# A two-layer adaLN transformer stack with a mixture of experts: the experts' down products turned round, their gate moved to VectorE and the residual add to GpSimd

## The chip, the cores and the metric

The kernel runs on one core of one Trainium2 chip. The metric is the device time of one execution in microseconds, lower is better. Inside the core work TensorE (PE, with its weight loads shown apart as PEld), VectorE (DVE), ScalarE (ACT), GpSimd (POOL) and SyncE (SP), which here only issues DMAs.

## The reference, cut to what matters

Thirty-two samples of 256 tokens with 128 features pass through two layers, each an attention and a feed-forward part with a residual around it. The change is in the feed-forward part of the first layer, a mixture of experts:

```
h = layernorm(x) * (1 + cb) + sb                       # cb, sb, gb: one row of 128 per sample
combine = router(h)                                    # 4 of 16 experts per token, weights
routed = sum over e of combine[:, e] * (relu(h @ up_w[e].T)**2 @ down_w[e].T)
shared = relu(h @ shared_up.T)**2 @ shared_down.T
x = x + gb * (routed + shared)                         # gb: the gate, per sample and feature
```

Each expert has 64 inner features, the shared expert 256, so there are 16*64 + 256 = 1280 inner features, or ten blocks of 128.

## The kernel before

The kernel is a row of stages, each a block with one hand-ordered instruction list per engine: a setup, `attention0` (prefix `a_`), `moe` (prefix `b_`), `attention1` (`c_`) and `mlp` (`d_`). The activations `x` stay in SBUF, a token on each partition: 64 tiles of 128 tokens by 128 features. The change touches `moe` alone.

`moe` makes `RUNS` = 16 runs `n`, each over two samples, that is 512 tokens or four tiles (`T4`). The features of these tokens stand on partitions after TensorE has turned them (`pe_front`), with the 512 tokens along the free axis. For each block `u` of the ten (0 and 1 are the shared expert, 2 to 9 the routed ones):

- `pe_up(n, u)`: one float32 product, the 128x128 up weights stationary, the 512 tokens moving, into one of four PSUM banks `pU`. A float32 product shows in the trace as two matmul records, each with a weight load of its own.
- `act_relu`, `act_square` (ScalarE): relu out of PSUM, then the square, into `q` (routed) or `a` (shared).
- `dve_weigh` (VectorE, routed blocks): `a = q * cwB`, where `cwB` holds each token's weight for the expert, spread over that expert's 64 partitions. These 2 MB per run come by DMA: VectorE writes `cwT`, SyncE sends it to DRAM (`by_expert`, four DMAs), waits for that to land, and fetches it back spread (`cwB`, four DMAs of 512 KB). `cwB` has two buffers.
- `pe_down(n, u)`: the down weights `dT` stationary, the 512 columns of `a` moving, added up over the ten blocks in the PSUM bank `pD`: features on partitions, tokens along the free axis.

After the tenth block ScalarE multiplies `pD` by the gate (`act_gate`, two instructions, one per sample, the gate as a per-partition scalar `c.mod[:, 0, 5, ...]`) into `og`; TensorE turns `og` back in four 128x128 transposes into `pB` (`pe_back`); VectorE adds `pB` to `x` (`dve_add`) and later measures mean and variance of the new `x` for the next layer norm (`dve_measure`, steps 1 and 2). `ln_scales` makes the reciprocal roots out of the variances.

The order on each engine is written out by hand and skewed: in pass `n` of the loop TensorE does the last three downs of run `n-1` between the first three ups of run `n`, then `pe_front(n+2)`, up 3, down 0, up 4, down 1, `pe_route(n+2)`, up 5, `pe_back(n-1)`, down 2, and so on in turns. `pe_down(n, 0)` waits until `pD` of run `n-1` has been read (`s_og`). On SyncE everything stands in one list: per run the `by_expert` DMAs, a wait, the `cwB` DMAs, and in run 2 also the loads of the last stage's weights (`ahead`).

Of the kernel before, what the change touches and what calls it, by code (L numbers as in the profile page):

```python
# [7 lines left out]
F32 = mybir.dt.float32  # L8
F16 = mybir.dt.float16
I32 = mybir.dt.int32  # L10
ALU = mybir.AluOpType
# [1176 lines left out]
def moe(nc, c, weights, ahead, halve, following, products):  # L1188
# [4 lines left out]
    with ExitStack() as ctx:  # L1193
# [31 lines left out]
        r, q, a = ([sb(f'{x}{k}', [P, W]) for k in range(4)] for x in ('r', 'q', 'a'))  # L1225
        og = sb('og', [D, W])
        pX, pR, pD, pB = (ctx.enter_context(nc.psum_tensor('b_p' + x, [P, BANK], F32)) for x in 'XRDB')
# [5 lines left out]
        s_up, s_r, s_sq, s_a, s_dn = (sem(x) for x in ('up', 'r', 'sq', 'a', 'dn'))  # L1233
        s_og, s_oT, s_st = (sem(x) for x in ('og', 'oT', 'st'))
        s_eT, s_pz, s_pT, s_pd, s_pm = (sem(x) for x in ('eT', 'pz', 'pT', 'pd', 'pm'))
        block = ctx.enter_context(nc.Block())

        @block.sync
        def _(sp):
            for n in range(RUNS):  # L1240
                sp.wait_ge(s_cT, n + 1)
                if n >= 1:
                    for part in s_cw:
                        sp.wait_ge(part, 2 * 16 * n)
                for t in range(T4):
                    sp.dma_start(by_expert[:, t, :], cwT[SQ * t:SQ * t + E, :, :].rearrange('e j r -> e (j r)')).then_inc(s_cd, 16)
# [40 lines left out]
        def pe_down(pe, n, u):  # L1287
            if u < ST:
                pe.wait_ge(s_sq, IT * n + u + 1)
            else:  # L1290
                pe.wait_ge(s_a, RT * n + u - ST + 1)
            if u == 0 and n >= 1:
                pe.wait_ge(s_og, n)
            t = weights_of(u)
            pe.matmul(pD[:, :], dT[:, t * D:(t + 1) * D], a[(IT * n + u) % 4][:, :], start=u == 0, stop=u == IT - 1).then_inc(s_dn, 1)  # L1295

        def pe_back(pe, n):
            pe.wait_ge(s_og, n + 1)
            if n >= 1:
                pe.wait_ge(s_st, ADD_STEPS * (n - 1) + 1)  # L1300
            for t in range(T4):
                last = pe.transpose(pB[:, t * P:(t + 1) * P], og[:, t * P:(t + 1) * P], c.id32[:, :])
            last.then_inc(s_oT, 1)

        @block.tensor
        def _(pe):
            for n in range(-2, RUNS + 1):
# [29 lines left out]
                if 0 <= n < RUNS:  # L1337
                    pe_up(pe, n, 5)
                if 0 <= n - 1 < RUNS:
                    pe_back(pe, n - 1)  # L1340
                if n == RUNS:
# [104 lines left out]

        def dve_add(dve, n):
            dve.wait_ge(s_oT, n + 1)
            add_to_x(dve, c, s_st, n, T4, pB[:, :])

# [4 lines left out]
        def _(dve):  # L1455
            dve.wait_ge(weights.s_loaded, 16 * MOE_LOADS)
            dve.wait_ge(s_km, 4)
            for n in range(-2, RUNS + 1):
                if 0 <= n - 1 < RUNS:
                    dve_weigh(dve, n - 1, 9)  # L1460
                if n == RUNS:
                    dve.wait_ge(s_st, ADD_STEPS * (RUNS - 1))
                    ln_scales(dve, c, s_ln, LN_STEPS, slice(0, TILES - T4))
                if n < 1 and n + 1 >= 0:
# [6 lines left out]
                elif 1 <= n < RUNS - 2:  # L1471
                    dve_normalise(dve, n + 2)
                if 1 <= n and n + 1 < RUNS:
                    dve_weights(dve, n + 1)
                if 0 <= n < RUNS:
                    dve_weigh(dve, n, 2)
                    dve_weigh(dve, n, 3)
                    dve_weigh(dve, n, 4)
                if 0 <= n - 1 < RUNS:
                    dve_add(dve, n - 1)  # L1480
                if 0 <= n < RUNS:
# [11 lines left out]
                if 0 <= n - 1 < RUNS:  # L1493
                    dve_measure(dve, n - 1, 2)
                if 0 <= n + 2 < RUNS:
                    dve_group_ranks(dve, n + 2)
# [40 lines left out]

        def act_gate(act, n):
            if n >= 1:
                act.wait_ge(s_oT, n)  # L1540
            act.wait_ge(s_dn, IT * (n + 1))
            for m in range(S2):
                last = act.activation(og[:, m * N:(m + 1) * N], pD[:, m * N:(m + 1) * N], ACT.Copy, scale=c.mod[:, 0, 5, n * S2 + m:n * S2 + m + 1])
            last.then_inc(s_og, 1)

        @block.scalar
        def _(act):
            for n in range(-2, RUNS + 1):
                if 0 <= n < RUNS:
# [4 lines left out]
                    act_relu(act, n, 2)  # L1554
                if 0 <= n - 1 < RUNS:
                    act_gate(act, n - 1)
                if n == RUNS:
# [17 lines left out]
                if 5 <= n < 5 + MLP_HALVES:  # L1575
                    halve(act, n - 5)
                if 0 <= n < RUNS:
                    act_square(act, n, 5)
# [11 lines left out]
        def _(gp):  # L1590
# [10 lines left out]
            gp.wait_ge(s_pz, 3)  # L1601
            attention1_spread(gp, following, products)


# [880 lines left out]
```

## Time and profile before

| | |
|---|---|
| time, median of 3 runs | 1916.07 us (1915.91 to 1919.06) |
| profiled execution | 1918.4 us, its span 1916.7 us |
| busy share of the span | PE 97%, PEld 68%, DVE 82%, ACT 75%, POOL 36% |
| stage `moe` | from about 884 to 1202.9 us of the span |
| granted clock of TensorE, mean | 0.986 |

The span is the time from the first to the last instruction in the profile. Busy time is the time in which an engine had at least one instruction in flight; a matmul's record includes its way through the array, so records of neighbouring matmuls overlap, and the rate is read from their starts.

### The profile page before, as it was taken

To read this page: it belongs to the slowest core of one execution; us is meant where nothing else is said; L and a number is where in the kernel's file an instruction comes from. 1 tells how busy PE (TensorE), PEld (TensorE's weight loads), DVE (VectorE), ACT (ScalarE), POOL (GpSimd) and SP (SyncE) were. 2 spreads that over 40 slices of the span, in tenths; PEclk is the share of its full clock that TensorE was granted. 3 is DMA by queue.
4 is the path that set the end of the run, shared out by engine and by line. 5 is a ranking of instruction groups with operands and counts; after the bars stand their busy time and mean duration, and the time that the engine had idled before them with its cause. 6 is when DMAs were issued, how large, how long until landed. Compare 5 with 4: busy or idle time off the path is not lost. (4 is left out here: it accounts for less than half of the span.)

```text
span 1916.7 us, 41298 instructions
## 1 busy us (share of the span) xinstructions
PE 1860.9 (97%) x14878; PEld 1297.1 (68%) x14878; DVE 1568.7 (82%) x3859; ACT 1437.4 (75%) x2026; POOL 684.3 (36%) x956
## 2 busy tenths in 40 slices
PE   7999999999999999998999999899999979999998
PEld 4788888888888888885444444677777754444443
DVE  7888888888888888865767775699999978888886
ACT  3888888888888888875677776566677766666665
POOL 2555656655656655551000000355555530000000
PEclk8999999999999999999999999999999989999999
DMA  3501111101111101111765544100000000000000
GB/s 101 130 19 29 29 29 29 29 18 26 29 29 29 29 21 23 27 23 39 169 142 114 121 105 87 45 2 2 2 2 2 2 2 6 12 17 12 12 17 17
DMA packets 62121, 75.68 MB, mean 39 GB/s; under 512 B 10480, under 2 KB 35168, under 8 KB 61792
## 3 DMA queue, kind: packets, MB, share of 16 engines
q1 hardware_dynamic: 61920, 73.03, 16.3%
q8 instruction: 122, 2.00, 0.4%
q14 instruction: 79, 0.65, 0.1%
HBM read 51.47 MB, written 4.77 MB: 29 GB/s over the span
## 5 line engine op out<-in xcount | busy, mean ns | idle before, releaser
L531 PE MATMUL a_pS<-qs,k 128*128 128x256 f16 x1536 | 415.3, 273 | 2.5 <-ACT th L1004 2.3
L551 PEld LDWEIGHTS a_pO<-va,pr 128*128 128x128 f32 x2048 | 312.6, 191 | 61.9 <-issue 58.4
L551 PE MATMUL a_pO<-va,pr 128*128 128x66 f32 x2048 | 322.0, 249 | 1.6 <-POOL pr L1086 1.1
L1004 ACT ACTIVATE th<-a_pS 128x1536 f32<-128x1536 f32 x128 | 185.4, 1449 | 89.7 <-PE a_pS L531 89.6
L531 PEld LDWEIGHTS a_pS<-qs,k 128*128 128x128 f16 x1536 | 223.5, 146 | 4.1 <-issue 2.2
L1978 ACT ACTIVATE c_pr<-c_pS 128x2048 f32<-128x2048 f32 x96 | 180.3, 1879 | 58.6 <-PE c_pS L1786 58.6
L2033 POOL TENSOR_SCALAR_AFFINE_SELECT c_pr<-c_pr 128x512 f32<-128x512 f32 x256 | 154.9, 635 | 180.1 <-DVE c_pr L1880 180.1
L1086 POOL TENSOR_SCALAR_AFFINE_SELECT pr<-pr 128x512 f32<-128x512 f32 x256 | 156.3, 634 | 176.0 <-ACT pr L1012 175.7
L1012 ACT ACTIVATE pr<-th 128x1536 f32<-128x1536 f32 x128 | 190.0, 1485 | 1.1
L797 DVE TENSOR_TENSOR qg<-a_pW,a_gam 128x512 f32<-128x512 f32 x192 | 131.8, 687 | 66.2 <-ACT sq L968 62.5
L867 POOL TENSOR_TENSOR qp<-qg,qp 128x1024 f16<-128x1024 f32 x64 | 139.2, 2175 | 126.7 <-ACT qp L980 126.7
L1097 POOL TENSOR_TENSOR as<-on 128x128 f32<-128x128 f32 x256 | 162.2, 635 | 55.9 <-DVE on L860 55.2
L553 PE MATMUL a_pO<-va,pr 128*128 128x66 f32 x1024 | 171.9, 249 | 0.0
L1295 PE MATMUL b_pD<-b_a,b_dn 128*128 128x512 f32 x320 | 165.8, 604 | 4.0 <-DVE b_a L1445 3.5
L553 PEld LDWEIGHTS a_pO<-va,pr 128*128 128x128 f32 x1024 | 157.0, 191 | 14.3 <-issue 14.3
L1285 PE MATMUL b_pU<-b_hT,b_un 128*128 128x512 f32 x320 | 163.7, 597 | 0.0
L1445 DVE TENSOR_TENSOR b_a<-b_q,b_cwB 128x512 f32<-128x512 f32 x128 | 87.8, 688 | 73.4 <-ACT b_q L1536 61.9
L1523 ACT ACTIVATE b_r<-b_pU 128x512 f32<-128x512 f32 x160 | 95.5, 597 | 68.5 <-PE b_pU L1285 68.5
L1880 DVE TENSOR_SCALAR c_pr<-c_pr 128x2048 f32<-128x2048 f32 x96 | 116.3, 1211 | 26.4 <-ACT c_pr L1978 26.4
L451 PE MATMUL a_pW<-a_wq,hT 128*128 128x512 f32 x256 | 132.4, 600 | 0.9 <-DVE qg L797 0.6
L2178 PE MATMUL d_pH<-d_a,d_h1T 128*128 128x512 f16 x512 | 122.1, 381 | 2.7 <-DVE d_a L2290 2.7
L968 ACT ACTIVATE sq<-a_pW 128x512 f32<-128x512 f32 x192 | 110.8, 596 | 15.3 <-PE a_pW L451 10.4
(267 smaller groups left out, 4245.6 us busy)
## 6 DMA issues: line engine op xcount, KB each, us to landing
b_cwB<-b_by_expert SPq DMA_DIRECT2D x64, 512.0 KB, 8.5
k<-k SPq DMA_DIRECT2D x128, 128.0 KB, 2.3
x<-in_L_attn_tokens_dram SPq DMA_DIRECT2D x8, 512.0 KB, 6.9
out_dram<-x SPq DMA_DIRECT2D x16, 256.0 KB, 2.3
mb<-a_by_sample SPq DMA_DIRECT2D x31, 128.0 KB, 3.3
d_h<-in_L_ffn_h_w_dram SPq DMA_DIRECT2D x2, 1024.0 KB, 8.3
c_gb<-c_by_sample SPq DMA_DIRECT2D x1, 2048.0 KB, 6.7
b_by_expert<-b_cwT SPq DMA_DIRECT2D x64, 8.0 KB, 1.5
```

The source lines that it names most:

```text
L531: last = pe.matmul(out, (k1, k2)[part][k][:, keys, h // G2, :], q, start=part == 0, stop=part == 1)
L551: last = pe.matmul(out, w[:, hh * N + t * P:hh * N + (t + 1) * P], v[:, 0, p, :], start=True, stop=t == 0)
L553: last = pe.matmul(out, w[:, HPG * N + hh * P:HPG * N + (hh + 1) * P], v[:, 1, p, :], start=False, stop=True)
L867: eng.tensor_tensor(to[:, t, :, DH:2 * DH], x.rearrange('p (h d) -> p h d', d=DH), to[:, t, :, 0:DH], ALU.subtract).then_inc(done, 1)
L1004: act.activation(th[:, :], pS[:, :], ACT.Tanh, scale=1.0 / SOFTCLAMP).then_inc(s_th, 1)
L1012: act.activation(pr[g % 2][:, :], th[:, :], ACT.Exp, scale=SOFTCLAMP * DH ** (-0.5)).then_inc(s_pr, 1)
L1086: last = gp.affine_select(out=own, in_=own, compare_op=ALU.is_ge, fill=0.0, base=0, pattern=[[0, HPG], [1, P]], channel_multiplier=-1)
L1097: gp.tensor_tensor(as_[:, :, p * DH:(p + 1) * DH], o[:, :, 0, :], o[:, :, 1, :], ALU.add).then_inc(s_as, 1)
L1285: pe.matmul(pU[(IT * n + u) % 4][:, :], uT[:, t, :], hT[n % 3][:, :], start=True, stop=True).then_inc(s_up, 1)
L1295: pe.matmul(pD[:, :], dT[:, t * D:(t + 1) * D], a[(IT * n + u) % 4][:, :], start=u == 0, stop=u == IT - 1).then_inc(s_dn, 1)
L1978: act.activation(pr[(3 * n + b) % NB][:, :, :], pS[:, :, :], ACT.Exp, scale=float(1.0 / np.sqrt(np.float32(DQ)))).then_inc(s_ex, 1)
L2033: gp.affine_select(out=part, in_=part, compare_op=ALU.is_ge, fill=0.0, base=0, pattern=[[0, HPG], [1, P]], channel_multiplier=-1).then_inc ...
```

## The change

The down product is turned round: the activations `a` become stationary, four tiles of 128 tokens each, and the down weights move, 128 columns. One `pe_down` is now four float32 products of 128 columns where it was one of 512; the sum in `pD` stands in token rows, as `x` does. `pe_back` and its transposes are gone. The gate is no longer one scalar per partition, but a row per sample along the free axis: TensorE turns the gates once (`pe_turn_gates`, in pass -1), ScalarE copies them (`act_take_gates`), SyncE sends them to DRAM at run 1 and fetches them per run spread over all partitions (`sp_load_gates`, 128 KB into `gr`, two buffers). VectorE multiplies `pD` by `gr` into `og` (`dve_gate`), and GpSimd adds `og` to `x` (`add`; the last run's is VectorE's). The `ln_scales` of the first 60 tiles moves behind the last measure.

```diff
-        og = sb('og', [D, W])
+        og = sb('og', [P, T4, D])
+        gates, gr = og[0:B, 0, :], [sb(f'gr{k}', [P, S2, D]) for k in range(2)]
+        GATES_OUT = 18
+        gate_rows = nc.dram_tensor('b_gate_rows', (B, D), F32, kind='Internal').ap()
...
+        def sp_load_gates(sp, n):
+            if n >= 2:
+                sp.wait_ge(s_og, n - 1)
+            sp.wait_ge(s_gr, GATES_OUT + 16 * n)
+            sp.dma_start(gr[n % 2][:, :, :].rearrange('p m d -> p (m d)'),
+                         gate_rows[n * S2:(n + 1) * S2].rearrange('m d -> (m d)').partition_broadcast(P)).then_inc(s_gr, 16)
...
             for n in range(RUNS):
+                if n == 1:
+                    sp.wait_ge(s_gr, 2)
+                    sp.dma_start(gate_rows, gates).then_inc(s_gr, 16)
+                    sp_load_gates(sp, 0)
+                if n >= 1:
+                    sp_load_gates(sp, n)
                 sp.wait_ge(s_cT, n + 1)
...
-            pe.matmul(pD[:, :], dT[:, t * D:(t + 1) * D], a[(IT * n + u) % 4][:, :], start=u == 0, stop=u == IT - 1).then_inc(s_dn, 1)
-
-        def pe_back(pe, n):
-            pe.wait_ge(s_og, n + 1)
-            if n >= 1:
-                pe.wait_ge(s_st, ADD_STEPS * (n - 1) + 1)
-            for t in range(T4):
-                last = pe.transpose(pB[:, t * P:(t + 1) * P], og[:, t * P:(t + 1) * P], c.id32[:, :])
-            last.then_inc(s_oT, 1)
+            for k in range(T4):
+                last = pe.matmul(pD[:, k * D:(k + 1) * D], a[(IT * n + u) % 4][:, k * P:(k + 1) * P], dT[:, t * D:(t + 1) * D],
+                                 start=u == 0 and k == 0, stop=u == IT - 1 and k == T4 - 1)
+            last.then_inc(s_dn, 1)
+
+        def pe_turn_gates(pe):
+            pe.transpose(pB[0:B, 0:D], c.mod[:, 0, 5, :], c.id32[:, :]).then_inc(s_gr, 1)
...
-        def dve_add(dve, n):
-            dve.wait_ge(s_oT, n + 1)
-            add_to_x(dve, c, s_st, n, T4, pB[:, :])
+        def dve_gate(dve, n):
+            dve.wait_ge(s_dn, IT * (n + 1))
+            dve.wait_ge(s_gr, GATES_OUT + 16 * (n + 1))
+            if n >= 1:
+                dve.wait_ge(s_st, ADD_STEPS * (n - 1) + 1)
+            dve.tensor_tensor(og[:, :, :].rearrange('p (m t) d -> p m t d', t=TT), pD[:, :].rearrange('p (m t d) -> p m t d', m=S2, t=TT),
+                              gr[n % 2][:, :, :].unsqueeze(2).broadcast_to((P, S2, TT, D)), ALU.mult).then_inc(s_og, 1)
+
+        def add(eng, n):
+            eng.wait_ge(s_og, n + 1)
+            if n >= 1:
+                eng.wait_ge(s_st, ADD_STEPS * n)
+            xt = c.x[:, n * T4:(n + 1) * T4, :]
+            eng.tensor_tensor(xt, xt, og[:, :, :], ALU.add).then_inc(s_st, 1)
...
-        def act_gate(act, n):
-            if n >= 1:
-                act.wait_ge(s_oT, n)
-            act.wait_ge(s_dn, IT * (n + 1))
-            for m in range(S2):
-                last = act.activation(og[:, m * N:(m + 1) * N], pD[:, m * N:(m + 1) * N], ACT.Copy, scale=c.mod[:, 0, 5, n * S2 + m:n * S2 + m + 1])
-            last.then_inc(s_og, 1)
...
             attention1_spread(gp, following, products)
+            for n in range(RUNS - 1):
+                add(gp, n)
```

On TensorE the middle of a pass reads as follows before the change; `b_pU` is an up product, `b_pD` a down, `b_pX` the turned tokens of the run after next, `b_pR` the router's product and `b_pB` the back transposes.

```order
L1266 MATMUL b_pX<-id,b_xn 128x128 x4
L1285 MATMUL b_pU<-b_hT,b_un 128x512
L1295 MATMUL b_pD<-b_a,b_dn 128x512
L1285 MATMUL b_pU<-b_hT,b_un 128x512
L1295 MATMUL b_pD<-b_a,b_dn 128x512
L1276 MATMUL b_pR<-b_hT,b_gT 32x128 x4
L1285 MATMUL b_pU<-b_hT,b_un 128x512
L1302 MATMUL b_pB<-id,b_og 128x128 x4
L1295 MATMUL b_pD<-b_a,b_dn 128x512
```

The same place of the changed kernel:

```order
L1282 MATMUL b_pX<-id,b_xn 128x128 x4
L1301 MATMUL b_pU<-b_hT,b_un 128x512
L1312 MATMUL b_pD<-b_dn,b_a 128x128 x4
L1301 MATMUL b_pU<-b_hT,b_un 128x512
L1312 MATMUL b_pD<-b_dn,b_a 128x128 x4
L1292 MATMUL b_pR<-b_hT,b_gT 32x128 x4
L1301 MATMUL b_pU<-b_hT,b_un 128x512
L1312 MATMUL b_pD<-b_dn,b_a 128x128 x4
```

The four transposes are gone, and each down stands as four products of 128 columns at the place of the one of 512.

On VectorE, at the start of a pass before the change, `b_xn` is the normalised run after next, `b_cw` to `b_cwT` the expert weights of the next run, `b_a` the weighing:

```order
L112 TENSOR_SCALAR b_xn<-x,mv,rs 128x128 x4
L1425 SCALAR_TENSOR_TENSOR b_cw<-b_rep,b_s 128x64
L1427 TENSOR_REDUCE b_tot<-b_cw 128x4
L1429 TENSOR_SCALAR b_tot<-b_tot 128x4
L1431 RECIPROCAL b_tot<-b_tot 128x4
L1433 SCALAR_TENSOR_TENSOR b_cwp<-b_cw,b_tot 128x4x16
L1437 STREAM_TRANSPOSE b_cwT<-b_cwp 128x128
L1445 TENSOR_TENSOR b_a<-b_q,b_cwB 128x512 x3
L128 TENSOR_TENSOR x<-x,b_pB 128x512
```

In the changed kernel:

```order
L112 TENSOR_SCALAR b_xn<-x,mv,rs 128x128 x4
L1466 TENSOR_TENSOR b_og<-b_pD,b_gr 128x512
L1439 SCALAR_TENSOR_TENSOR b_cw<-b_rep,b_s 128x64
L1441 TENSOR_REDUCE b_tot<-b_cw 128x4
L1443 TENSOR_SCALAR b_tot<-b_tot 128x4
L1445 RECIPROCAL b_tot<-b_tot 128x4
L1447 SCALAR_TENSOR_TENSOR b_cwp<-b_cw,b_tot 128x4x16
L1451 STREAM_TRANSPOSE b_cwT<-b_cwp 128x128
L1459 TENSOR_TENSOR b_a<-b_q,b_cwB 128x512 x4
```

The gate stands ahead of the six instructions that make `cwT`, so these now come after the wait for the last down; the add behind the third weighing is gone.

On SyncE the first runs before the change:

```order
L1246 DMA b_by_expert<-b_cwT 16x128 x4
L1253 DMA b_cwB<-b_by_expert 64x4x512 x4
L1246 DMA b_by_expert<-b_cwT 16x128 x4
L1253 DMA b_cwB<-b_by_expert 64x4x512 x4
L1246 DMA b_by_expert<-b_cwT 16x128 x4
L1253 DMA b_cwB<-b_by_expert 64x4x512 x4
```

And in the changed kernel:

```order
L1262 DMA b_by_expert<-b_cwT 16x128 x4
L1269 DMA b_cwB<-b_by_expert 64x4x512 x4
L1253 DMA b_gate_rows<-b_og 32x128
L1245 DMA b_gr<-b_gate_rows 128x256 x2
L1262 DMA b_by_expert<-b_cwT 16x128 x4
L1269 DMA b_cwB<-b_by_expert 64x4x512 x4
L1245 DMA b_gr<-b_gate_rows 128x256
L1262 DMA b_by_expert<-b_cwT 16x128 x4
L1269 DMA b_cwB<-b_by_expert 64x4x512 x4
```

Ahead of run 1's expert weights now stand the gate rows' way out and two fetches, each of which waits for the one before it to land; ahead of every later run's stands one fetch.

## Rows read from the trace of the kernel before

**Rows 1.** Windows: us, then each engine's busy time, TensorE clock, DMA share

```profile
908.00:916.00 8.00, 6.59 (x9) 2.80 (x10) 6.30 (x20) 2.43 (x4) 0.00 (x0) 0.57 0.54 106
1008.00:1026.00 18.00, 18.00 (x56) 8.10 (x55) 12.94 (x53) 13.62 (x26) 0.00 (x0) 1.00 0.62 129
```

**Rows 2.** Timeline, TensorE, one pass: start, duration, engine, line, operation

```profile
1014.14 1.02 PE L1295 MATMUL b_pD<-b_a,b_dn 128*128 128x512 f32 x2
1015.00 0.60 PE L1266 MATMUL b_pX<-id,b_xn 128*128 128x128 f32 x4
...
1020.30 0.60 PE L1302 MATMUL b_pB<-id,b_og 128*128 128x128 f32 x4
1020.74 1.02 PE L1295 MATMUL b_pD<-b_a,b_dn 128*128 128x512 f32 x2
...
1033.62 0.60 PE L1266 MATMUL b_pX<-id,b_xn 128*128 128x128 f32 x4
```

**Rows 3.** Timeline, ScalarE and VectorE, the same pass

```profile
1015.26 0.84 ACT L1543 ACTIVATE b_og<-b_pD,mod 128x256 f32<-128x256 f32 x2 [0.32 <-PE b_pD L1295]
...
1012.48 1.11 DVE L112 TENSOR_SCALAR b_xn<-x,mv,rs 128x128 f32<-128x128 f32 x4
1013.50 0.22 DVE L1425 SCALAR_TENSOR_TENSOR b_cw<-b_rep,b_s 128x64 f32<-128x64 f32 x1
...
1016.65 0.69 DVE L1445 TENSOR_TENSOR b_a<-b_q,b_cwB 128x512 f32<-128x512 f32 x1 [1.65 <-ACT b_q L1536]
```

**Rows 4.** Timeline, TensorE in attention1: two products of 128 columns in turn

```profile
1307.66 0.63 PEld L1775 LDWEIGHTS c_pC<-c_wv,c_hT 128*128 128x128 f32 x4
1307.87 0.61 PE L1775 MATMUL c_pC<-c_wv,c_hT 128*128 128x128 f32 x4
```

**Rows 5.** Timeline, SyncE's queue: start, time to issue, DMAs

```profile
913.28 1.71 SPq L1246 DMA_DIRECT2D b_by_expert<-b_cwT  x4
916.06 2.56 SPq L1253 DMA_DIRECT2D b_cwB<-b_by_expert  x4
...
954.03 2.57 SPq L1253 DMA_DIRECT2D b_cwB<-b_by_expert  x4
...
1017.80 2.56 SPq L1253 DMA_DIRECT2D b_cwB<-b_by_expert  x4
```

**Rows 6.** DMA issues: KB each, median us from issue to landing

```profile
mb<-a_by_sample SPq DMA_DIRECT2D x31, 128.0 KB, 3.3
```

**Rows 7.** Timeline, VectorE and TensorE, runs 1 and 3: weighings that waited for cwB

```profile
923.66 0.69 DVE L1445 TENSOR_TENSOR b_a<-b_q,b_cwB 128x512 f32<-128x512 f32 x1 [2.03 <-DMA b_cwB<-b_by_expert]
...
961.95 1.44 DVE L1445 TENSOR_TENSOR b_a<-b_q,b_cwB 128x512 f32<-128x512 f32 x2 [3.35 <-DMA b_cwB<-b_by_expert]
...
927.20 0.60 PE L1302 MATMUL b_pB<-id,b_og 128*128 128x128 f32 x4
...
964.44 0.60 PE L1302 MATMUL b_pB<-id,b_og 128*128 128x128 f32 x4
```

**Rows 8.** Groups by line, GpSimd: count, busy us, mean ns

```profile
L867 POOL TENSOR_TENSOR qp<-qg,qp 128x1024 f16<-128x1024 f32 x64 | 139.2, 2175 | 126.7 <-ACT qp L980 126.7
L128 POOL TENSOR_TENSOR x<-x,c_og 128x256 f32<-128x256 f32 x32 | 28.4, 887 | 5.1 <-DVE c_og L1914 5.1
```

**Rows 9.** Timeline, ScalarE and VectorE, end of the stage

```profile
1197.78 0.84 ACT L1543 ACTIVATE b_og<-b_pD,mod 128x256 f32<-128x256 f32 x2 [2.23 <-PE b_pD L1295]
...
1201.93 0.69 ACT L1676 ACTIVATE c_wq<-b_pU 128x16 f32<-128x16 f32 x4
...
1196.18 0.18 DVE L88 TENSOR_SCALAR var<-mv 128x60 f32<-128x60 f32 x1
...
1198.16 0.22 DVE L104 SCALAR_TENSOR_TENSOR rs<-ln_half,rs 128x60 f32<-128x60 f32 x1
1199.43 0.69 DVE L128 TENSOR_TENSOR x<-x,b_pB 128x512 f32<-128x512 f32 x1 [1.05 <-PE b_pB L1302]
...
1201.06 0.38 DVE L140 BATCH_NORM_AGGREGATE mv<-stat 128x2 f32<-128x6 f32 x4
```

More of the change, by code:

```diff
@@ L1233, in moe @@
         s_up, s_r, s_sq, s_a, s_dn = (sem(x) for x in ('up', 'r', 'sq', 'a', 'dn'))
-        s_og, s_oT, s_st = (sem(x) for x in ('og', 'oT', 'st'))
+        s_og, s_st, s_gr = (sem(x) for x in ('og', 'st', 'gr'))
         s_eT, s_pz, s_pT, s_pd, s_pm = (sem(x) for x in ('eT', 'pz', 'pT', 'pd', 'pm'))
         block = ctx.enter_context(nc.Block())
+        def sp_load_gates(sp, n):
[4 more added lines that the diff above has]
+                         gate_rows[n * S2:(n + 1) * S2].rearrange('m d -> (m d)').partition_broadcast(P)).then_inc(s_gr, 16)
         @block.sync
@@ L1338, in _ @@
                     pe_up(pe, n, 5)
-                if 0 <= n - 1 < RUNS:
-                    pe_back(pe, n - 1)
+                if n == -1:
+                    pe_turn_gates(pe)
                 if n == RUNS:
@@ L1460, in _ @@
                     dve_weigh(dve, n - 1, 9)
-                if n == RUNS:
-                    dve.wait_ge(s_st, ADD_STEPS * (RUNS - 1))
-                    ln_scales(dve, c, s_ln, LN_STEPS, slice(0, TILES - T4))
                 if n < 1 and n + 1 >= 0:
@@ L1472, in _ @@
                     dve_normalise(dve, n + 2)
+                if 0 <= n - 1 < RUNS:
+                    dve_gate(dve, n - 1)
+                if n == RUNS:
+                    add(dve, RUNS - 1)
                 if 1 <= n and n + 1 < RUNS:
@@ L1478, in _ @@
                     dve_weigh(dve, n, 4)
-                if 0 <= n - 1 < RUNS:
-                    dve_add(dve, n - 1)
                 if 0 <= n < RUNS:
@@ L1494, in _ @@
                     dve_measure(dve, n - 1, 2)
+                if n == RUNS:
+                    dve.wait_ge(s_st, ADD_STEPS * (RUNS - 1))
+                    ln_scales(dve, c, s_ln, LN_STEPS, slice(0, TILES - T4))
                 if 0 <= n + 2 < RUNS:
@@ L1536, in act_square, with act_take_gates @@
             act.activation(to[:, :], r[(IT * n + u) % 4][:, :], ACT.Square).then_inc(s_sq, 1)
-        def act_gate(act, n):
-            if n >= 1:
-                act.wait_ge(s_oT, n)
-            act.wait_ge(s_dn, IT * (n + 1))
-            for m in range(S2):
-                last = act.activation(og[:, m * N:(m + 1) * N], pD[:, m * N:(m + 1) * N], ACT.Copy, scale=c.mod[:, 0, 5, n * S2 + m:n * S2 + m + 1])
-            last.then_inc(s_og, 1)
+        def act_take_gates(act):
+            act.wait_ge(s_gr, 1)
+            act.activation(gates, pB[0:B, 0:D], ACT.Copy).then_inc(s_gr, 1)
         @block.scalar
@@ L1554, in _ @@
                     act_relu(act, n, 2)
-                if 0 <= n - 1 < RUNS:
-                    act_gate(act, n - 1)
                 if n == RUNS:
@@ L1576, in _ @@
                     halve(act, n - 5)
+                if n == -1:
+                    act_take_gates(act)
                 if 0 <= n < RUNS:
```

## The prediction

> **What bounds the kernel now.** The change touches one stage, so the first view is the table of busy time by stretch. In an 18 us stretch of the stage TensorE is busy for all 18.00 us at a granted clock of 1.00, while VectorE works 12.94, ScalarE 13.62 and GpSimd nothing [rows 1]. The second view is the timeline of one pass: from one group of `b_pX` transposes at 1015.00 to the next at 1033.62 it is 18.62 us, with no idle time on TensorE between [rows 2]. So the stage's length is the sum of what TensorE issues; an instruction taken from ScalarE or VectorE is worth nothing in itself, and one put on them costs nothing while its result is there when TensorE asks. The third view is SyncE's queue, since the waits for `cwB` in the first runs are the only ones near TensorE's needs [rows 5, 7].
>
> A record's duration must not be added up here, since records overlap: a down shows 1.02 us, but the next group starts 0.86 us after it (1014.14 to 1015.00), and that is what it costs. The four back transposes cost 1020.74 - 1020.30 = 0.44 us [rows 2].
>
> **The back transposes go.** Passes 1 to 15 hold one group each: 15 x 0.44 = **-6.6 us**. The sixteenth stands at the stage's end and is counted there.
>
> **The downs.** One down was two records of 512 columns and becomes eight of 128, each with a weight load of 128x128 float32. Before, the load hid behind the 512 columns of the record ahead. Now load and matmul are about equally long, and the question is what one costs next to the other. The nearest row is in attention1: four records of 128 columns with fresh float32 weights, not transposes, take 0.61 us from the first start to the last end, one record being 0.275 long, so they start every (0.61 - 0.275)/3 = 0.112 us; their loads show (0.63 - 0.19)/3 = 0.147, of which the first wait, for the 256-column record ahead, takes the excess [rows 4]. The transposes give (0.60 - 0.273)/3 = 0.109 us, as their own loads are lighter [rows 2]. I take 0.112, since it is the same operation in form and type: 8 x 0.112 = 0.896 against 0.86, or 0.036 more per down. For 160 downs that is **+5.8 us**. Below, 0.109 gives 0.872 and +1.9; above stands the case that nothing is hidden (second rival).
>
> **The gate on VectorE.** ScalarE began the gate at 1015.26 and needed 0.84 us [rows 3]. VectorE multiplies 512 columns in 0.69 [rows 3], with a source in PSUM too [rows 9], and is free from 1015.00 on, so it ends at about 1015.95, 0.15 us sooner. `pe_down(n, 0)`, which waits for it, loses nothing. Queued behind the gate are the six instructions for `cwT`, which took from 1013.50 to 1015.00 [rows 3] and now run from 1015.95 to 1017.45; then the weighing for down 2, done at 1018.15. TensorE asks for it where the transposes stood, 1020.30: 2.1 us of cover. `cwT` itself is 2.45 us late, and with the 128 KB gate fetch ahead of it `cwB` starts about 3 us later than 1017.80 [rows 5]; it is needed in the next pass, some 17 us on, and its first half comes within 7.6 us (below). **0**. ScalarE's lost 0.84 us were under TensorE: **0**.
>
> **The add on GpSimd.** GpSimd is idle here. Its two-input add takes 0.887 us for 256 columns and 2.175 for 1024 [rows 8], so some 1.3 for 512. `dve_measure` wants it only behind four weighings of 0.69 that start at 1017.45, so from 1020.2 on; the add is done by 1017.3: **0**. If its ports hold VectorE up while it runs, the weighing at 1018.15 slips to 1019.45, still before 1020.30: the hold decides from 2.1 us on. The Trainium skill ("SBUF — State Buffer", port pair shared by VectorE and GpSimd) says that a GpSimd instruction and a VectorE one with two SBUF inputs lock each other out fully; by that the slip is the whole add, and still zero in the sum.
>
> **The gate rows' way round.** This is the new wait. SyncE's list is in order. At run 1 it used to start the `by_expert` DMAs at 913.28, as soon as run 0's `cwB` had landed [rows 5]. Now three steps come first: `gate_rows` goes out, queued behind run 0's `cwB` and so landing at about that same moment, some 0.3 to 1 us later; the fetch of run 0's rows waits for it and lands, as the like 128 KB spread does, in 3.3 us [rows 6]; the second fetch is issued (0.6 us, as one of the four `cwB` DMAs in 2.56 [rows 5]) and the `by_expert` DMAs queue behind its data. Sum 4.2 us; bounds 3.0 (both landings short) and 5.0. So run 1's `cwB` starts at 920.3, not 916.06. VectorE's first weighing of run 1 was released 7.6 us after the issue, at 923.66 [rows 5, 7]; now 927.9, result at 928.6. TensorE wants it at 927.2 plus 0.2 for longer downs, where the transposes stood [rows 7]: a stall of 1.2 us.
>
> The queue then stays dense through the loads for the last stage: run 3's `cwB` was issued at 954.03, and its weighing began at 961.95 [rows 5, 7]. With 4.2 us inherited, the issue and data of two more fetches (1.1), and 0.74 for the weighing, the result is there at 968.0. TensorE wants it at 964.44, less two groups of transposes (0.9), plus 25 longer downs (0.9) and the 1.2 already lost: 965.6. A stall of 2.4. Both together are the inherited delay less 0.6: **+3.6 us** (2.4 to 4.4). By run 4 the queue has caught up, as each run's chain is shorter than a pass.
>
> **The end.** VectorE gates at 1197.78, where ScalarE did, to 1198.5, and adds. Add and measures took from 1199.43 to 1201.44, 2.0 us, so they end at 1200.5. The nine `ln_scales` steps, which were done at 1198.4 under the wait, now follow: 2.2 us, 1202.7. The other end of the stage, ScalarE's copies, was at 1202.6 and comes earlier, freed of the gate [rows 9]. **+0.1**. The one transpose of the gates falls in the start, where TensorE waits for the first `cwB` anyway (busy 6.59 of 8 us even as it ends [rows 1]): 0.
>
> **Sum.** -6.6 + 5.8 + 3.6 + 0.1 = +2.9; the gate's 0.15 us gives back a few hundredths per pass that down 0 now waits, -0.2 in all: **+2.7 us**. The profiled execution took 1918.4 us for a span of 1916.7, 2.3 above the median; the terms are differences and carry over, so the forecast is 1916.1 + 2.7 = **1918.8**, by the bound of 0.2% (3.8 us), which is about what a measurement of this kernel can tell from no change, the same.
>
> **Rivals.**
> *It gets faster (14%).* The fetches land early or the delay is used up by slack I don't see, and the records start every 0.109 us: -6.6 + 1.9 + 0 to 1 = -4.7 to -3.7, 1911.5 to 1912.5. For it: transposes at 0.109 all through this stage. Against it: both attention1 products, float32 weights, at 0.112, and the 3.3 us row. It decides if the stalls stay under 1 us.
> *The loads aren't hidden (4%).* A load of about 0.11 and a matmul of 0.107 in turn make 0.22 per record, 1.75 per down, +0.89 x 160 = +143 us, 2060. The attention1 rows speak against it: 0.112. The Trainium skill ("TensorE: Matmul & The Clock Gate", on what overlaps when small matmuls are packed) says that a load overlaps a matmul in flight only when its row group differs, and here all use the same rows; by that this rival would be the forecast. The trace disagrees, for these four records and for every down before.
> *The stall brings the clock down (24%).* After TensorE waited for run 0's `cwB`, the granted clock was 0.57 of full over 908 to 916 [rows 1]. If the 2.4 us stall in run 3 does the same, 8 us at 0.57 cost 8 x 0.43 = 3.4 us: 2.7 + 3.4 = +6.1, 1922.2, slower. For it: the stall is alike. Against: that wait was longer, with another one just before.
> *VectorE or the queue late in every pass (4%).* If GpSimd's hold goes past 2.1 us by 1, each pass loses 1: +15, 1933.
> The forecast itself: 54%.
>
> **From these the numbers.** The likeliest case alone spans 1913.8 (0.109 and short stalls: -6.6 + 1.9 + 2.4 = -2.3) to 1919.6 (long stalls, +0.8). The range reaches into the clock case: 1913.8 to 1923.2. Slower by over 0.2%: the clock, the loads, VectorE, 0.32. Faster 0.14. Same 0.54.
>
> **What the changed profile would show.** Eight records per down, starting every 0.112 us, and a steady pass of 18.62 - 0.44 + 0.36 = 18.5 us with TensorE still always busy; `cwB` of run 1 issued at about 920; TensorE waiting for `b_a` once in run 1 and once in run 3, 3.6 us together, and the clock row there at 1.00; GpSimd's add near 1.3 us; the stage's end set by `ln_scales`. The forecast fails if records start every 0.107 or 0.12, if the granted clock falls at run 3, or if each pass shows idle time on TensorE before down 2.

## The result and the profile after

The changed kernel took 1924.21 us (median of 20 executions, 1918.76 to 1932.34) against 1918.94 us for the kernel before in the same measurements (20, 1915.91 to 1925.48). The ratio is 1.0022, 95% interval 1.0012 to 1.0032: slower by 0.2%, about 4.2 us; the two medians lie 5.3 us apart, 0.27%, which is inside the interval. By the 4.2 us, added to the time before that the forecast started from (1916.07), it is 1920.3 us, in the upper half of the forecast range; the median of these 20 executions itself, which has a slower kernel before beside it, is 1.0 us above the range's end. Of the cases it is not the likeliest but the third rival, the one with the falling clock, and a second loss that the forecast did not have.

The profiled execution has a span of 1922.0 us, 5.3 more than before. Cut at TensorE's first record of the stage and at the first of the next one (`attention1`): 883.2 us before the stage instead of 884.7 (unchanged code; a second profile of the kernel before had 883.4), 323.3 in it instead of 318.2, and 715.4 behind it instead of 713.8.

The steady pass is the first thing to look at. Windows of the changed kernel (us, then busy time of PE, PEld, DVE, ACT and POOL with counts, TensorE's granted clock, DMA share, GB/s), one over a steady stretch, one over run 1 and one over run 3:

```profile
1008.00:1026.00 18.00, 18.00 (x110) 12.97 (x109) 14.11 (x57) 13.00 (x23) 1.27 (x1) 1.00 0.60 127
924.00:930.00 6.00, 4.71 (x34) 3.08 (x33) 3.38 (x7) 3.03 (x8) 0.00 (x0) 1.00 1.06 207
966.00:974.00 8.00, 5.93 (x26) 4.42 (x27) 5.57 (x18) 1.69 (x3) 0.00 (x0) 0.79 0.74 146
```

TensorE is as full as before in the steady stretch [rows 1], so the sum over its instructions still holds there. In run 1 and run 3 it is not full, and in run 3 its clock is below 1.00.

Timeline of TensorE in the changed kernel: a pass, and the two waits with what released them.

```profile
1020.00 0.60 PE L1282 MATMUL b_pX<-id,b_xn 128*128 128x128 f32 x4
...
1021.29 1.05 PE L1312 MATMUL b_pD<-b_dn,b_a 128*128 128x128 f32 x8
1022.18 1.02 PE L1301 MATMUL b_pU<-b_hT,b_un 128*128 128x512 f32 x2
...
1038.50 0.60 PE L1282 MATMUL b_pX<-id,b_xn 128*128 128x128 f32 x4
...
927.30 1.16 PE L1312 MATMUL b_pD<-b_dn,b_a 128*128 128x128 f32 x8 [1.29 <-DVE b_a L1459]
...
968.07 1.77 PE L1312 MATMUL b_pD<-b_dn,b_a 128*128 128x128 f32 x8 [3.49 <-DVE b_a L1459]
969.63 1.92 PE L1301 MATMUL b_pU<-b_hT,b_un 128*128 128x512 f32 x2
```

A pass is 18.50 us (1020.00 to 1038.50) where it was 18.62 [rows 2]; a down takes 1022.18 - 1021.29 = 0.89 us for eight records, 0.11 between starts: (1.05 - 0.28) / 7 = 0.11. The waits are for the weighed activations, 1.29 us in run 1 and 3.49 in run 3, and behind the second an up product shows 1.92 us where it has 1.02 at full clock. The pass with run 3's wait, from the `b_pX` at 959.06 to the one at 982.99, is 23.93 us long: 18.50, the wait of 3.49, and 1.94 more, most of it the lower clock (behind the wait of 1.29, where the clock stayed, the same difference is 0.3 us).

Why the weighing is late stands in SyncE's queue of the changed kernel (start, time to issue):

```profile
902.02 0.77 SPq L1253 DMA_DIRECT2D b_gate_rows<-b_og  x1
912.26 3.43 SPq L1245 DMA_DIRECT2D b_gr<-b_gate_rows  x2
915.80 1.75 SPq L1262 DMA_DIRECT2D b_by_expert<-b_cwT  x4
918.99 2.56 SPq L1269 DMA_DIRECT2D b_cwB<-b_by_expert  x4
...
931.45 1.96 SPq L1262 DMA_DIRECT2D b_by_expert<-b_cwT  x4
935.97 2.56 SPq L1269 DMA_DIRECT2D b_cwB<-b_by_expert  x4
...
959.66 2.56 SPq L1269 DMA_DIRECT2D b_cwB<-b_by_expert  x4
```

These stand beside [rows 5], where 1.5 us must be added to a start here, since the stage begins that much sooner. The gate rows are issued at 902.02, but the first fetch only at 912.26, when they have landed behind run 0's expert weights. These ten microseconds are not the price: `by_expert` of run 1 waits for run 0's `cwB` anyway, and started at 913.28 before the change, where the first fetch now starts at 912.26 + 1.5 = 913.7. The rest are the two fetches, one after the other, from 912.26 to 915.80. `by_expert` of run 1 starts at 915.80 + 1.5 = 917.3 instead of 913.28, 4.0 us late; `cwB` of run 1 at 920.5 instead of 916.06, of run 3 at 961.1 instead of 954.03, which is 7.1 us late.

VectorE and GpSimd in a steady pass, changed kernel:

```profile
1020.20 0.69 DVE L1466 TENSOR_TENSOR b_og<-b_pD,b_gr 128x512 f32<-128x512 f32 x1 [1.46 <-PE b_pD L1312]
...
1021.31 0.96 DVE L1443 TENSOR_SCALAR b_tot<-b_tot 128x4 f32<-128x4 f32 x1
...
1020.97 1.27 POOL L1474 TENSOR_TENSOR x<-x,b_og 128x512 f32<-128x512 f32 x1 [17.23 <-DVE b_og L1466]
```

The gate takes 0.69 us and the add 1.27, as forecast. The small `tensor_scalar` on four columns shows 0.96 us, and ends with GpSimd's add (1022.24). The `tensor_reduce` that began under the same add, at 1021.05, took its usual 0.22 us. No VectorE instruction with two inputs in SBUF begins under the add in a steady pass.

And the end of the stage, VectorE, ScalarE and TensorE of the changed kernel, then the windows behind the seam, one of the changed kernel and one of the kernel before:

```profile
1201.92 0.69 DVE L1474 TENSOR_TENSOR x<-x,b_og 128x512 f32<-128x512 f32 x1
...
1203.56 0.38 DVE L140 BATCH_NORM_AGGREGATE mv<-stat 128x2 f32<-128x6 f32 x4
...
1205.81 0.22 DVE L104 SCALAR_TENSOR_TENSOR rs<-ln_half,rs 128x60 f32<-128x60 f32 x1
...
1204.54 0.67 ACT L1701 ACTIVATE c_wq<-b_pU 128x16 f32<-128x16 f32 x4
...
1206.57 0.37 PE L1843 MATMUL c_pC<-id,mod 128*32 128x128 f32 x1 [3.63 <-PEq L1193]
```

```profile
1204.00:1217.00 13.00, 8.49 (x41) 6.08 (x42) 4.73 (x15) 2.41 (x19) 2.51 (x6) 0.50 0.39 163
```

```profile
1202.00:1209.00 7.00, 4.21 (x11) 2.89 (x11) 2.82 (x5) 1.45 (x10) 2.36 (x6) 0.51 0.46 190
1209.00:1216.00 7.00, 4.11 (x40) 3.12 (x38) 2.58 (x5) 2.46 (x3) 0.00 (x0) 1.00 0.27 112
```

ScalarE's copies end at 1205.2, `ln_scales` at 1206.0; TensorE waits 3.63 us for the next stage. Behind it the clock stands at 0.50 for all of 13 us; before the change it was back at 1.00 after 7.

### The profile page after: what moved, and what is told of

Same layout as the page of the kernel before. It is cut to its first block and busy times, and to the rows that moved or that the text cites. A ratio compares the mean times of both kernels' runs of the same rounds, so it can differ in the third digit from the quotient of the medians.

```text
span 1922.0 us, 43109 instructions
## 1 busy us (share of the span) xinstructions
PE 1861.8 (97%) x15775; PEld 1380.2 (72%) x15775; DVE 1577.7 (82%) x3860; ACT 1427.9 (74%) x1995; POOL 703.8 (37%) x971
## 5 line engine op out<-in xcount | busy, mean ns | idle before, releaser
L1312 PEld LDWEIGHTS b_pD<-b_dn,b_a 128*128 128x128 f32 x1280 | 170.2, 195 | 83.1 <-issue 62.5
L1312 PE MATMUL b_pD<-b_dn,b_a 128*128 128x128 f32 x1280 | 171.7, 279 | 8.2 <-DVE b_a L1459 8.2
```

The costliest lines, as they stand in the source:

```text
L1312: last = pe.matmul(pD[:, k * D:(k + 1) * D], a[(IT * n + u) % 4][:, k * P:(k + 1) * P], dT[:, t * D:(t + 1) * D], start=u == 0 and k == 0, ...
```

## The experiments

Ratios are to the kernel before in the same series of measurements, with 95% intervals; two versions of different series are compared by these ratios. "The wait" is TensorE's.

One thing must be known before the profiles are compared. In every version TensorE waits 2.8 to 4.2 us for run 0's expert weights, and behind that wait the clock is low for a time that varies from execution to execution. The five downs there, in e5 and in e6, which are the same kernel up to the seam (the place where `moe` ends and `attention1` begins):

```profile
907.63 7.65 PE L1313 MATMUL b_pD<-b_dn,b_a 128*128 128x128 f32 x40 [3.31 <-DVE b_a L1459]
908.45 6.36 PE L1313 MATMUL b_pD<-b_dn,b_a 128*128 128x128 f32 x40 [2.88 <-DVE b_a L1460]
```

They took 7.3 to 7.7 us in both profiles of the kernel before, in the changed kernel, e1, e2, e5 and e10, 6.9 to 7.2 in the changed kernel's second profile, e3 and e4, and 6.3 to 6.4 in e6 to e9. So a stage can be 1.3 us shorter by this alone, and TensorE then asks for run 3's weights that much sooner.

**e1: the gates early.** In SyncE's list:

```diff
-                if n == 1:
+                if n == 0:
                     sp.wait_ge(s_gr, 2)
                     sp.dma_start(gate_rows, gates).then_inc(s_gr, 16)
                     sp_load_gates(sp, 0)
-                if n >= 1:
+                    sp_load_gates(sp, 1)
+                if n >= 2:
                     sp_load_gates(sp, n)
```

with `pe_turn_gates` and `act_take_gates` moved to the start of the stage.

> The changed kernel, with the gates turned and copied at the start of the stage and their way to DRAM and the first two fetches issued before run 0's expert weights, where the queue is empty, instead of between run 0's and run 1's. Theory (the gate rows' way round delays the expert weights): TensorE's waits in run 1 (1.29 us) and run 3 (3.49 us) both go, and the granted clock stays at 1.00 through run 3 (it fell for 3.4 us, worth about 1.7): 6.5 us less than the changed kernel, so about -1.2 us against the kernel before (ratio 0.999). Steady pass unchanged at 18.50 us. Rival (the waits come from the later passes' fetches, or from expert weights computed later behind the gate): waits stay, time stays within 1 us of the changed kernel, ratio 1.002.

Measured: 1918.29 us against 1918.04, ratio 0.9999 (0.9988 to 1.0010). The intervals of this kernel and the changed one don't meet: the late gates cost 0.23%, some 4.4 us, where 6.5 had been expected. Windows of e1 over run 1, run 3 and behind the seam:

```profile
924.00:930.00 6.00, 6.00 (x43) 4.25 (x42) 3.99 (x13) 4.09 (x8) 0.00 (x0) 1.00 0.44 85
964.00:972.00 8.00, 8.00 (x46) 5.69 (x45) 7.31 (x36) 5.43 (x10) 0.00 (x0) 1.00 0.41 93
...
1197.00:1210.00 13.00, 7.78 (x39) 5.48 (x40) 5.26 (x15) 2.04 (x18) 2.36 (x6) 0.50 0.42 163
```

Both waits and the clock's fall are gone, the stage takes 316.7 us, 6.6 less than in the changed kernel and 1.5 less than before the change. VectorE's order with the gate ahead of the expert weights is unchanged here, so it is not what made the waits. But the kernel as a whole is not faster than before; behind the seam this profile has 717.3 us, at half clock for 13 us.

**e2: the fetches alone, in the kernel before.** The same DMAs at the same places of SyncE's list, from a cleared buffer into two that nobody reads:

```diff
+                if n == 1:
+                    sp.wait_ge(s_k, 2)
+                    sp.dma_start(gate_rows, gsrc[:, :]).then_inc(s_k, 16)
+                    sp_load_gates(sp, 0)
+                if n >= 1:
+                    sp_load_gates(sp, n)
                 sp.wait_ge(s_cT, n + 1)
```

> The kernel before, with the same DMAs as the changed one at the same places of SyncE's list (gate rows out at run 1, two fetches there, one per later run), into buffers that nobody reads; downs, gate and back transposes are as before. Theory: the queue alone makes the waits. TensorE's need is later here by the transposes (0.44 us a pass), so the wait in run 1 is about 0.9 us, in run 3 about 3.0, with or without the clock's fall: +4 to +6 us against before (ratio 1.002 to 1.003). Rival: the waits need the changed order on VectorE; then no wait and ratio 1.000.

Measured: 1925.72 us, ratio 1.0040 (1.0026 to 1.0054). In the profile the waits are 0.88 us in run 1, 0.62 in run 2 and 1.22 in run 3, 2.7 together (groups of waits: sum in us, count, longest):

```profile
PE b_pD L1310 <- DVE b_a L1460: 2.7, 3, 1.2
```

The queue alone makes waits, without any change on VectorE or TensorE. That in run 1 came as expected (0.9), that in run 3 did not (3.0 expected), and that in run 2 was not foreseen; the clock did not fall behind any of them. The time is larger than these waits and above what was expected: the stage is 3.7 us longer, and another 2.7 lie behind the seam, at a mean clock of 0.68 over 1203 to 1224 us. Why that part is there in this kernel, whose end of the stage is as before, stays open.

**e3: the downs in four, in the kernel before.** Stationary weights as before, loaded for each quarter:

```diff
-            pe.matmul(pD[:, :], dT[:, t * D:(t + 1) * D], a[(IT * n + u) % 4][:, :], start=u == 0, stop=u == IT - 1).then_inc(s_dn, 1)
+            for k in range(T4):
+                last = pe.matmul(pD[:, k * P:(k + 1) * P], dT[:, t * D:(t + 1) * D], a[(IT * n + u) % 4][:, k * P:(k + 1) * P],
+                                 start=u == 0 and k == 0, stop=u == IT - 1 and k == T4 - 1)
+            last.then_inc(s_dn, 1)
```

> The kernel before, each down product split into four of 128 columns with the same stationary weights, loaded anew for each; nothing else changed. Theory (a record of 128 columns is bound by its 0.112 us load): a down costs 0.89 us instead of 0.86, a pass 18.62 + 0.34 = 18.96 us, +5.5 us against before, ratio 1.0029. Rival (the cost belongs to the activations as stationary operand, or to short records' issue): if only activations as weights cost it, ratio 1.000; if it is issue, more than +6.

Measured: 1924.94 us, ratio 1.0042 (1.0030 to 1.0055). Its passes:

```profile
1018.25 0.60 PE L1266 MATMUL b_pX<-id,b_xn 128*128 128x128 f32 x4
...
1037.22 0.60 PE L1266 MATMUL b_pX<-id,b_xn 128*128 128x128 f32 x4
```

18.97 us, 0.35 more than 18.62, as expected: the price is that of short records with a float32 load each, not of activations as weights. It is 16 x 0.35 = 5.6 us of the 8 measured; the stage is 4.9 us longer in the profile (the five downs behind run 0's wait were 0.6 us shorter in this execution), and the remainder lies in unchanged stages, where this execution's clock was 0.53 over 11 us behind the seam. Whether it is the load or something else in a short record that sets the 0.112 us is not shown: a quarter of the 0.43 us of a 512-column record is 0.107, so what comes on top is 0.005 us a record.

**e4: the first two fetches together.** No wait for the first to land before the second is issued (`if n != 1` ahead of the wait in `sp_load_gates`, and the gate of run 0 waits for both).

> The changed kernel, with the second fetch of run 1 issued without waiting for the first to land. Theory: the delay of run 1's by_expert DMAs falls from about 4 us to about 1.5 (one landing of 2.3 us less), the wait in run 1 goes, that in run 3 shrinks from 3.49 to about 2.4 us or less (total waits = delay less a constant), 2.4 us less than the changed kernel, 4 if the clock no longer falls. Rival (the delay comes from the gate rows waiting behind run 0's expert weights, not from the fetches' landings): no difference.

Measured: 1923.27 us, ratio 1.0034 (1.0022 to 1.0046); the interval overlaps that of the changed kernel, so in time nothing is shown. The profile does answer. Run 1's `by_expert` starts 1.3 us later in the stage than before the change, not 4.0; there is no wait in run 1, one of 1.07 in run 3, and the clock there is at 1.00.

```profile
PE b_pD L1313 <- DVE b_a L1460: 1.1, 1, 1.1
```

The stage takes 317.2 us, 6.1 less than in the changed kernel, 3.7 of them waits and about 1.9 the clock in run 3, so the fetch's landing was the larger part of the delay. The same execution lost as much in unchanged code, 2.5 us ahead of the stage and 3.7 behind the seam, which is why the stage has to be read from the profile here.

**e5: as e1, with the scales at their old place**, `ln_scales` of the first 60 tiles ahead of the last gate.

> The changed kernel with the gates early, as in e1, and the ln_scales of the first 60 tiles back at their old place, right behind the last weighing and ahead of the last gate. Theory (the moved scales stretch the end of the stage, and with it TensorE's wait of 3.63 us at the seam to the next stage, which keeps the clock at half for longer there): the stage ends about 1.0 us earlier, the seam's wait is near 2.6 us, and the half-speed stretch after it is shorter than 13.7 us; 1 to 3 us less than e1, ratio 0.998 to 0.9995. Rival (the scales' place costs nothing, as ScalarE's copies end then anyway): ratio as e1, 1.000.

Measured: 1919.49 us, ratio 0.9995 (0.9983 to 1.0007). TensorE at the seam, and the windows behind it:

```profile
1198.53 0.37 PE L1842 MATMUL c_pC<-id,mod 128*32 128x128 f32 x1 [2.57 <-PEq L1193]
```

```profile
1197.00:1204.00 7.00, 4.32 (x11) 2.88 (x11) 2.77 (x10) 2.07 (x18) 2.51 (x6) 0.51 0.37 133
1204.00:1210.00 6.00, 4.03 (x40) 3.12 (x38) 2.59 (x5) 1.53 (x3) 0.00 (x0) 1.00 0.48 198
```

The wait is 2.57 again, the half-speed stretch 7 us again, and the profiled span 1911.7 against 1916.9 in e1. Over the timed executions the difference to e1 is 0.04%, less than the intervals: the shape at the seam is shown, its worth in time is not by this pair.

**e6 and e7: TensorE kept busy over the seam**, in e5 and in the kernel before:

```diff
                     attention1_multiply(pe, following, products, pU[1]).then_inc(s_pm, 1)
+                    keep_busy(pe, c, pU[2], 20)
```

> As e5, with 20 idle transposes of the identity on TensorE (2.2 us) behind its last products of the stage, while it would wait for the next stage; they write a bank that nobody reads. Theory (the half-speed stretch at the seam is what the rest of the kernel loses): the granted clock stays at 1.00 through the first products of attention1, or falls for one short stretch; 1.5 to 3.5 us less than e5, ratio against before about 0.997. Rival (the stretch is set by the waits inside attention1's first batch): same as e5.

> The kernel before, with the same 20 transposes at the same place. Theory: the seam's half-speed stretch (6.8 us before) goes too, 1 to 3 us less, ratio 0.9985 to 0.9995; the changed kernel loses more at this seam than the kernel before, so it gains more from them. Rival as in e6: 1.000.

Measured: e6 1916.31 us, ratio 0.9983 (0.9972 to 0.9994); e7 1918.75, ratio 1.0000 (0.9991 to 1.0009). Windows behind the seam, e6, then e7:

```profile
1197.00:1210.00 13.00, 8.68 (x69) 6.84 (x68) 6.51 (x19) 5.33 (x30) 2.51 (x6) 1.00 0.43 163
```

```profile
1200.00:1217.00 17.00, 12.15 (x76) 8.79 (x75) 6.35 (x11) 5.57 (x15) 4.32 (x9) 0.80 0.32 125
```

With the wait cut to 0.30 us the clock stays at 1.00 in e6. In the kernel before the same cut only moves the slow part: 0.80 over the 17 us, and no gain. So my expectation for e7 was wrong, and what e6 has over e5 is not settled as the seam's alone; the two intervals overlap. e6 shows a wait of 1.14 us in run 3 where e5 has none. That is no effect of the transposes: `cwB` of run 3 is issued 71.2 us into the stage in e6 and 71.3 in e5, but TensorE, after its shorter downs in run 0, began run 3's pass 1.2 us sooner.

**e8: as e1, with the add on VectorE** behind the third weighing.

> As e1, with the add on VectorE at its old place behind the third weighing of a pass instead of on GpSimd. Theory (VectorE is not asked for anything there by TensorE): VectorE's small tensor_scalar in the weights falls from 0.96 to 0.17 us, the pass stays at 18.50 us with TensorE always busy, time as e1, ratio 1.000. Rival (the move to GpSimd buys time): slower than e1 by up to 0.69 x 15 = 10 us, ratio 1.005.

Measured: 1920.48 us, ratio 1.0004 (0.9992 to 1.0016), as e1. VectorE's `tensor_scalar` and TensorE's passes:

```profile
1035.04 0.17 DVE L1443 TENSOR_SCALAR b_tot<-b_tot 128x4 f32<-128x4 f32 x1
```

```profile
1015.22 0.60 PE L1283 MATMUL b_pX<-id,b_xn 128*128 128x128 f32 x4
1033.73 0.60 PE L1283 MATMUL b_pX<-id,b_xn 128*128 128x128 f32 x4
```

0.17 instead of 0.96, and a pass of 18.51: the add on GpSimd holds VectorE up, and where it stands makes no difference to the time that this pair can tell. A wait of 1.83 us stood in run 3 of this profile, at a clock of 1.00.

**e9: as e6, each fetch behind its run's expert weights**, and VectorE's weights for the next run ahead of the gate.

```diff
-                if n >= 2:
-                    sp_load_gates(sp, n)
...
+                if n >= 2:
+                    sp_load_gates(sp, n)
                 if n == 2:
                     ahead(sp)
```

> As e6 (gates early, scales back, transposes over the seam), with each later run's gate fetch issued behind that run's expert weights instead of ahead of them, and on VectorE the weights of the next run ahead of the gate. Theory: in run 3 the expert weights no longer queue behind a fetch and come about 1.1 us earlier, so the wait of 1.14 us that e6 showed there goes, and none is left in the steady passes; up to 1.1 us less than e6, ratio 0.998 or just under. Rival (the wait in run 3 comes from the last stage's loads alone): as e6.

Measured: 1915.77 us against 1918.25, ratio 0.9978 (0.9966 to 0.9990), the lowest of all versions and clear of the kernel before, but with an interval that overlaps e6's. The run 3 wait is gone; two short ones for the gate came in its place in the early runs:

```profile
PE b_pD L1313 <- DVE b_og L1467: 0.8, 2, 0.6
```

`cwB` of run 3 was issued 0.8 us sooner than in e6, and the two short waits brought TensorE to it 0.5 us later, so both had a part. The edit also changed two things at once, the fetch's place and VectorE's order, and no run separates them.

**e10: the changed kernel with late gates, but the scales back and the seam closed.**

> The changed kernel with its late gates, but the scales at their old place and the 20 transposes over the seam. Theory (queue and seam are two separate losses that add): e6 plus the waits in runs 1 and 3 and the clock's fall there, 4.8 + 1.7 us: ratio 0.9983 + 0.0034 = 1.0017. Rival (the loss is all at the seam): ratio as e6, 0.998.

Measured: 1921.73 us, ratio 1.0011 (0.9999 to 1.0023). Against e6, which differs from it in the gates' time alone, the intervals don't meet: late gates cost 0.28% here, 5.4 us. The waits of runs 1 and 3 are there again, 1.32 and 4.22 us (groups of waits from 915 to 1190 us):

```profile
PE b_pD L1312 <- DVE b_a L1460: 5.5, 2, 4.2
```

**A second profile of both kernels.**

> The kernel before once more, for a second profile of the stage and of the seam behind it. If the half-speed stretch at the seam is set by the length of TensorE's wait, it is 6.8 us or near it again, and not 13.7 as in all three kernels that showed a wait of 3.6 us; if it is chance, any length.

> The changed kernel once more. Theory: waits in runs 1 and 3 again, 1.3 and 2 to 3.5 us, and 13.7 us at half speed behind the wait of 3.6 us at the seam. Rival (chance): no wait in one of the runs, or another stretch.

Measured, one execution each: 1917.15 and 1930.73 us. Windows behind the seam of the kernel before (first) and of the changed one, with run 3 of the latter:

```profile
1201.00:1208.00 7.00, 4.57 (x11) 2.88 (x11) 2.81 (x5) 1.10 (x6) 2.36 (x6) 0.52 0.52 185
1208.00:1215.00 7.00, 3.80 (x39) 3.12 (x38) 2.60 (x6) 2.72 (x3) 0.00 (x0) 1.00 0.27 117
```

```profile
1208.00:1222.00 14.00, 9.84 (x45) 7.16 (x46) 4.52 (x14) 2.10 (x14) 2.51 (x6) 0.51 0.39 152
969.00:976.00 7.00, 4.97 (x17) 3.94 (x18) 4.47 (x12) 1.12 (x2) 0.00 (x0) 0.51 0.84 164
```

The kernel before repeats itself. The changed kernel waited 1.77 and 4.63 us, more than expected, and its clock was at 0.51 for 7 us in run 3. This execution's span is 7.0 us longer than the first profile's: 1.8 ahead of the stage, 1.8 in it and 3.4 behind it. So run 3 is one place of the wide spread of its times (1918.8 to 1932.3), and not the largest in this execution.

**The seam over all profiles.** "Lost" is the sum of 1 minus the clock over 36 us, from 6 us ahead of `attention1`'s first record on:

| TensorE's wait at the seam | profiles | lost there, us | time behind the stage, us |
|---|---|---|---|
| 3.6 us | changed, its second profile, e1, e4, e8 | 6.8, 10.2, 6.8, 8.5, 10.2 | 715.4, 718.8, 717.3, 719.1, 719.5 |
| 2.57 us | before, its second profile, e5, e2, e3 | 3.4, 3.4, 3.4, 6.8, 5.1 | 713.8, 713.8, 713.2, 716.4, 716.6 |
| 0.30 us (20 transposes) | e6, e9, e10, e7 | 0, 0, 1.7, 3.4 | 711.3, 711.3, 714.5, 716.1 |

The time behind the stage, in code that no edit touches, goes with what the clock lost at the seam: 711.3 us where it lost nothing, 718.8 and 719.5 where it lost 10.2. What it lost grows with the wait in the main, but not strictly, since the groups overlap.

## Why the prediction came out as it did

As a difference to the kernel before, the time stands in the range; the likeliest case, no measurable change, did not come true by a little. The time alone does not decide between that case (+2.7 us, 0.14%) and the rival with the falling clock (+6.1, 0.32%), for both lie at the ends of the interval; the profile does. Point by point.

**Transposes and downs: right.** -6.6 + 5.8 made -0.8; from the pass it is 15 x (18.50 - 18.62) = -1.8, and the sixteenth run's downs, which have no such group beside them, give 0.3 back. The step was the choice of 0.112 us per record from attention1's four records, which every down of the changed kernel shows; only 0.86 + 0.036 should have been 0.86 + 0.033. e3 shows the price by itself. Without it the transposes would have been worth their 6.6 us; with it, turning the product round is nearly a trade. The rival without overlap of loads, and the rule of the Trainium skill ("TensorE: Matmul & The Clock Gate", on what overlaps when small matmuls are packed) that was named beside it, are contradicted by every down of the changed kernel: eight records within 1.05 us.

**Gate and add at nothing: right.** TensorE is busy for all of 18 us; e8 moves the add back with no change in time that the intervals show. The hold by GpSimd was seen, on the `tensor_scalar`, 0.8 us a pass, less than the 2.1 of cover. The prediction looked for it on a two-input weighing. In the changed kernel these meet the add once, in the last pass with an add: there the add, begun at 1186.77 under a weighing that had started at 1186.61, took 1.65 us instead of 1.27, and the next weighing, begun at 1188.15 in the add's last 0.27 us, took 0.81 instead of 0.69 (in e9, where the gate comes later, the add takes 1.65 in every steady pass). The Trainium skill ("SBUF — State Buffer", who interferes with whom) names `tensor_scalar` among the instructions that can contend for the pair, and says that `tensor_reduce` never does on this chip; the trace agrees with both, 0.96 us against 0.17 for the first and 0.22 either way for the second.

**The gate rows' way round: the mechanism right, its later part too small.** Forecast 4.2 us of delay and a wait of 1.2 in run 1: 4.0 and 1.29. Forecast 2.4 in run 3: 3.49, and 4.63 in the second profile. The term that failed is "the issue and data of two more fetches (1.1)": `cwB` of run 3 was 7.1 us late, not 5.3. The part shows in run 2, where `by_expert` to `cwB` took 935.97 - 931.45 = 4.5 us instead of 2.8 [rows 5], behind a fetch of 128 KB that I had priced at its bytes. How long that step takes is not fixed by the fetch alone: e2 and e4, with the same fetch at the same place, show 3.3 and 3.1 us there, and the second profile and e10 4.6 and 4.4; why, no run shows. e1 against the changed kernel and e6 against e10 show the cause by two pairs whose intervals don't meet (0.23% and 0.28%); e2 shows that the queue alone is enough for waits, though for 2.7 us of them and not 4.8.

**The clock: the rival, priced at 24%, came true.** In run 3 it fell in all three profiles with the changed kernel's queue (changed, second profile, e10), behind waits of 3.49, 4.63 and 4.22 us, and not behind 1.07, 1.14, 1.22 and 1.83 (e4, e6, e2, e8). That split was in no row of before. In the changed kernel it was short: 0.79 over 8 us costs 8 x 0.21 = 1.7 us, and 1.9 by the length of the pass, not the 3.4 forecast; in the second profile it was 7 us at 0.51, which is 3.4.

**The end: the step was wrong in what it left out.** "+0.1" was the stage's length, and that was about right. But I summed the stage and did not ask what TensorE does at the seam. ScalarE is freed of the gate, so TensorE's last products come sooner after the downs, and the scales let the next stage start later: its wait grew from 2.57 to 3.63 us, and with it the half-speed stretch from 7 to 13 us. In five profiles with the longer wait (changed, second profile, e1, e4, e8) it was 13 us or more, in three with 2.57 (before, second profile, e5) 7; e2 and e3, with 2.57 too, had slow parts of other lengths. That is a pattern with exceptions, not a law, and what sets the length is not shown. Its worth: e6 to e1 and e10 to the changed kernel each come out 0.11 to 0.16% faster, 2 to 3 us, but with intervals that overlap, and e7 gained nothing from the same 20 transposes.

**The sum in the profile.** Stage: -1.8 + 0.3 (passes) + 1.29 + 3.49 (waits) + 1.7 (clock) + 0.2 (end) = 5.2 against 5.1 seen; behind the seam 1.6. What keeps e1 from being faster than before, when its stage is 1.5 us shorter, is seen in its profile: 3.5 us more behind the seam, where the clock lost 3.4 more. That the longer wait at the seam causes this is argued, and not shown by time.

## What to carry to other kernels

On an engine that is always busy, count a product by the spacing of its records, and take that spacing from a row of the same form: here a record of 128 float32 columns with a load of its own took 0.112 us, where a quarter of a 512-column record is 0.107, so cutting a product in four cost 4% and ate most of what the saved transposes gave. A small DMA in an ordered list costs the time that its followers stand behind it, not its bytes: two fetches of 128 KB, each waiting for the one before it to land, held the list up for 3.5 us, and the gate rows' way to DRAM took ten microseconds behind 2 MB of weights but 2.4 in the empty queue of e1 (883.59 to 886.03). So put one-off round trips where the queue is empty. And a change in the last steps of a stage has to be read together with what the matmul engine does across the seam, for its clock may answer in the next stage. Last, look at an unchanged stretch of two profiles before you explain a difference of a microsecond between them: here one such stretch differed by 1.3 us.

## What the hardware showed

- A two-input add of 512 float32 columns on GpSimd takes 1.27 us, and a VectorE `tensor_scalar` on four columns that began under it took 0.96 us instead of 0.17. A `tensor_reduce` under it was not held (0.22). The hold goes both ways: with a two-input weighing on VectorE under way first, the add took 1.65 us.
- The granted clock fell from 1.00 to half behind a single wait of TensorE of 3.49 us or more in an otherwise full stretch, and didn't behind 1.83 or less.
- Behind the same seam the clock stood at 0.50 for 13 us in one profile of the changed kernel and at 0.51 for 14 in another, and the time behind the stage was 715.4 us in the first and 3.4 us more in the second. The second had another stretch at half clock, some 15 us behind the seam. Differences of 2 us are hard to time here.
